# A macaron block in one kernel: row transfers placed one iteration ahead and behind the scale, group products in three rounded parts

## What is computed

```python
x = x + 0.5 * ffn(layernorm(x), gate_w, gate_b, w1, w2)
x = x + attn(layernorm(x), Wq, bq, Wk, bk, Wv, bv, Wo, bo)
x = x + 0.5 * ffn(layernorm(x), gate_w, gate_b, w1, w2)

# ffn: 32 experts, each picks 8 tokens of every batch
probs = softmax(x @ gate_w.T + gate_b, over the tokens)
vals, idx = top_k(probs, 8)                  # per batch and expert
merged = sum over the 8 picks of vals * x[idx]
o = gelu([merged, 1] @ w1) ; o = [o, 1] @ w2 # one vector per batch and expert
out[idx] += o * vals                         # back to the picked tokens

# attn: 16 heads of 32, linear and causal
q, k = exp(x @ Wq.T + bq), exp(x @ Wk.T + bk) ; v = x @ Wv.T + bv
out = (q . cumsum(k v)) / (q . cumsum(k)) ; out = out @ Wo.T + bo
```

## Time and profile before

| what | value |
|---|---|
| median of 3 runs | 2286.3 (2284.62 to 2287.34) |
| the profiled execution | 2283.05, of which its span is 2281.3 |
| gate | 0 to about 145 |
| first expert pass | about 145 to 912 |
| attention | about 912 to 1641 |
| second expert pass and the end | about 1641 to 2281 |
| TensorE busy in the span | 1962.4 (86%) |
| granted TensorE clock, mean | 0.93 |
| DMA rate where its share is full | 427 to 429 GB/s |

### The profile page before, as it was taken

How to read it: one execution, slowest core, us unless ns; L and a number is a source line. 1 busy time by engine, 2 the same in 40 slices (tenths; PEclk the granted TensorE clock), 3 DMA queues, 4 the chain that set the end, 5 groups by cost and what they waited for, 6 DMA issues and landing times.

```text
span 2281.3 us, 43539 instructions
## 1 busy us (share of the span) xinstructions
PE 1962.4 (86%) x18440; PEld 1161.6 (51%) x18440; DVE 728.5 (32%) x1235; ACT 779.3 (34%) x1413; POOL 622.9 (27%) x756
## 2 busy tenths in 40 slices
PE   5789999999999999889999999999776566656667
PEld 4546666666666666666777776777521111111111
DVE  6731111111111111367777677677410000000011
ACT  6831111121111111357777777677510000000000
POOL 7610000000000000267777777777412000000002
PEclk9999999999999999999999999999897867787777
DMA  9999999999999999776776676676499999999997
GB/s 366 357 398 404 418 401 428 430 426 422 427 418 429 418 423 415 219 261 212 250 262 224 229 249 214 198 258 209 184 406 425 427 399 428 428 428 428 428 427 332
DMA packets 133202, 804.49 MB, mean 353 GB/s; under 512 B 31240, under 2 KB 31368, under 8 KB 91792
## 3 DMA queue, kind: packets, MB, share of 16 engines
q1 hardware_dynamic: 116880, 713.29, 79.0%
q10 hardware_dynamic: 9216, 50.34, 5.3%
q0 software_dynamic: 6912, 38.07, 4.3%
HBM read 678.24 MB, written 136.95 MB: 357 GB/s over the span
## 4 chain that ended last, share of the span: by engine, by line
PE 59%; DMA 24%; ACT 5%; POOL 5%; issue 4%; SPq 1%; DVE 1%; POOLq 0%; DVEq 0%; ACTq 0%
PE ps L349 54%; DMA big<-in_L_ffn_w 22%; PE ps L353 3%; SPq L18 1%; DMA last_scratch<-idx 1%; ACT big L635 1%; POOL big L1599 1%; POOL s L1602 1%; ACT big L620 1%; PE ps L824 1%; POOL big L1572 1%; ACT big L625 1%; DMA row_scratch<-idx 1%; PE ps L512 0%; ACT big L1391 0%
## 5 line engine op out<-in xcount | busy, mean ns | idle before, releaser
L349 PE MATMUL ps<-big 128*32 128x512 f32 (+5 forms) x13568 | 946.7, 412 | 229.9 <-DMA big<-in_L_ffn_w 179.9
L349 PEld LDWEIGHTS ps<-big 128*32 128x32 f32 (+2 forms) x13568 | 374.1, 126 | 727.4 <-issue 383.6
L357 DVE TENSOR_TENSOR big<-ps,big 128x128 f32<-128x128 f32 (+4 forms) x277 | 266.7, 966 | 697.9 <-PE ps L824 511.6
L349 PE MATMUL ps<-wth,xth 128*128 128x512 f32 x768 | 311.8, 406 | 1.5 <-DVE xtl L357 1.5
L349 PE MATMUL ps<-wtl,xth 128*128 128x512 f32 x768 | 299.6, 390 | 0.0
L349 PE MATMUL ps<-wth,xtl 128*128 128x512 f32 x768 | 299.3, 390 | 0.0
L872 ACT COPY big<-ps 128x512 f32<-128x512 f32 x64 | 37.5, 586 | 644.1 <-PE ps L349 623.3
L1544 POOL TENSOR_SCALAR big<-big 128x1 f32<-128x1 f32 x8 | 1.5, 188 | 827.6 <-ACT ps L1351 827.2
L1024 DVE TENSOR_SCALAR big<-ps,big 128x512 f32<-128x512 f32 x64 | 48.1, 751 | 533.7 <-PE ps L349 533.7
L1015 ACT ACTIVATE big<-ps,big 128x512 f32<-128x512 f32 x128 | 88.2, 689 | 371.8 <-PE ps L349 356.1
L349 PE MATMUL ps<-wo,s 128*128 128x512 f32 x768 | 210.0, 408 | 3.0 <-ACT s L1436 1.4
(11 more groups left out here) (140 smaller groups left out, 1761.8 us busy)
## 6 DMA issues: line engine op xcount, KB each, us to landing
big<-in_L_ffn_w SPq DMA_DIRECT2D x254, 2048.0 KB, 35.9
p_weight_x_scratch<-big ACTq DMA_DIRECT2D x64, 768.0 KB, 11.2
big<-p_weight_x_scratch SPq DMA_DIRECT2D x64, 768.0 KB, 5.7
xt_scratch<-big SPq DMA_DIRECT2D x16, 1024.0 KB, 8.6
big<-xt_scratch SPq DMA_DIRECT2D x16, 1024.0 KB, 16.2
x_weight_scratch<-big SPq DMA_DIRECT2D x64, 256.0 KB, 3.2
out_x<-big SPq DMA_DIRECT2D x64, 256.0 KB, 4.0
big<-in_L_attn_x SPq DMA_DIRECT2D x15, 1024.0 KB, 11.3
```

The costliest lines, as they stand in the source:

```text
L349: return nc.tensor.matmul(o, l, r, start=start, stop=stop, skip_group_check=True)
L357: return nc.vector.tensor_tensor(o, p, q, op)
```

## The change

Five things are edited. First, the gathers and scatters stand behind `scale_pool` at the end of GpSimd's iteration, instead of ahead of L1599. Second, their iterations are one earlier for the first gather and for the scatters: `turn` gives 8b - 13, 8b - 12 for the gathers, 8b - 10 for the weights, 8b - 9 and 8b - 8 for the products, and 8b - 8 and 8b - 7 for the scatters; the waits of the gathers on earlier scatters follow. For batch 1 the whole chain is one or two iterations earlier: gathers at -2, weights at -1, products at 0 and 1, scatters at 0 and 1. Third, from batch 2 on the products take rounded operands: ScalarE rounds OS to OSH and VectorE forms the rest OSL (`rows_outer_act`, `rows_outer_dve`, both in iteration 8b - 11, c = 5), VectorE writes the weights rounded and their rest (GWP), and TensorE adds three products, high by high, high by low and low by high, where it had one. Fourth, TensorE's wait for ScalarE's squares stands only before the products. Fifth, the part of `rows_sp` that waits for the written row numbers and reads them back is a function of its own, `rows_read_sp`, called at expert 8.

```diff
--- before.py
+++ after.py
@@ -145,7 +145,10 @@
         assert s.at == 4 * SLOT
         TILED = 1
         G = [at(w_at + 2 * SLOT - 64 + XP * i, XP) for i in range(2)]
-        GWT = [[at(p + 128 * i, 128) for i in range(2)] for p in (m_at + 2048, os_at)]
+        GWT = [at(m_at + 2048 + 128 * i, 128) for i in range(2)]
+        OSL = [halves(f"osl{b}", os_at + 512 * b, 512) for b in range(8)]
+        OSH = [None, None] + [halves(f"osh{b}", os_at + 512 * (b - 1), 512) for b in range(2, 8)]
+        GWP = [halves(f"gwp{i}", os_at + 256 * i, 256) for i in range(2)]
         MTK = [at(m_at + 2048 + 256 * b, 256).rearrange("p (c e) -> p c e", c=8) for b in range(8)]
         RANK1, POS = at(b_at - 1024, 1024), at(os_at, 1024)
         n3 = Area(hid_at)
@@ -265,6 +268,8 @@
         s_pos, PO0 = s_ve4, NG
         s_gwT, GT0 = s_tp4, 4 * NG
         s_gwt, GW0 = s_nm4, NG
+        s_osh, OH0 = s_nma, NG + NG // 2
+        s_osl, OL0 = s_ocl, 2
         s_gc, GC0 = s_lg4, NG
         s_ga, GA0 = s_nmd, NG
         s_xst, XS0 = s_bst4, 4 * NG
@@ -277,9 +282,9 @@
         d_g, d_s = d_pick[0], d_fs
 
         def turn(n, after):
-            if n == (-1, -1, 0, 1, 2, 2, 3)[after]:
+            if n == (-2, -2, -1, 0, 1, 0, 1)[after]:
                 return 1
-            b, k = divmod(n + 12 - after, 8)
+            b, k = divmod(n + 12 - (-1, 0, 2, 3, 4, 4, 5)[after], 8)
             return b if k == 0 and 2 <= b < B else None
 
         def slot_of(g):
@@ -788,6 +793,8 @@
                         load_chunk(sp, g + ahead)
                 if p == 0 and e == 6:
                     rows_sp(sp)
+                if p == 0 and e == 8:
+                    rows_read_sp(sp)
                 if p == 1 and e == 8:
                     last_rows_sp(sp)
                 if p == 0 and e % 2 == 0 and 2 <= e // 2 + 1 < NT // 4:
@@ -1204,7 +1211,8 @@
                 pe.wait_ge(s_st, n + 1)
                 for s_ in (s_tk, s_tqv):
                     pe.wait_ge(s_, min(n + 3, 8 * TILED))
-                pe.wait_ge(s_x1sq, min(n + 3, 8 * TILED))
+                if turn(n, 3) or turn(n, 4):
+                    pe.wait_ge(s_x1sq, min(n + 3, 8 * TILED))
                 if turn(n, 2):
                     rows_weights_pe(pe, turn(n, 2))
                 for i in range(2):
@@ -1231,7 +1239,7 @@
                     for s_ in (s_tk, s_tqv):
                         pe.wait_ge(s_, min(n + 2, 8 * TILED))
                     if turn(n - 1, 2):
-                        pe.wait_ge(s_gwt, GW0 + turn(n - 1, 2) - TILED + 1)
+                        pe.wait_ge(s_gwt, gwts(turn(n - 1, 2)))
                     for k in range(2):
                         if turn(n - 1, 3 + k):
                             pe.wait_ge(s_ga, GA0 + 2 * (turn(n - 1, 3 + k) - TILED) + k + 1)
@@ -1334,7 +1342,7 @@
                     pe.wait_ge(s_xt3, n - 1)
                     bank1(n)
                     transpose4(1, PB[m % 4][:, 0, :]).then_inc(s_qtT, 1)
-                if 0 <= n < 8 * TILED - 2:
+                if -1 <= n < 8 * TILED - 2:
                     rows_turn_pe(n)
                 if live:
                     pe.wait_ge(s_kt, min(n + 2, NT))
@@ -1416,6 +1424,8 @@
                     act.wait_ge(s_x2ve, t - 1)
                     nc.scalar.activation(ps[:, 0, :], X2, ACT.Square, bias=SX2[t % 2], scale=-float(D),
                                          accum_out=SQ2[t % 2]).then_inc(s_x2sq, 1)
+                if n >= 0 and turn(n - 1, 1):
+                    rows_outer_act(act, turn(n - 1, 1))
                 if n >= 14 and c == 6:
                     merge_tokens_act(act, 8 + (n - 14) // 8, 1)
                 if n >= 5 and n % 4 == 1 and n - 2 < NT:
@@ -1511,6 +1521,8 @@
                     dve.wait_ge(d_pb[m % 4], 16 * (m // 4 + 1))
                     tt(PB[m % 4][:, 0::2, :], ps[:, 4:7:2, :], PB[m % 4][:, 0::2, :], ALU.add).then_inc(s_tqv, 1)
                     tt(PB[m % 4][:, 1, :], ps[:, 5, :], PB[m % 4][:, 1, :], ALU.add).then_inc(s_tk, 1)
+                if n >= 0 and turn(n - 1, 1):
+                    rows_outer_dve(dve, turn(n - 1, 1))
                 if turn(n, 2):
                     rows_weights_dve(dve, turn(n, 2))
                 for i in range(2):
@@ -1581,12 +1593,6 @@
                     pool.wait_ge(s_nm, n)
                     pool.wait_ge(s_qn, min(n + 2, NT))
                     nc.gpsimd.tensor_tensor(ATL, AT, ATH.bitcast(F), ALU.subtract).then_inc(s_atl, 1)
-                for i in range(2):
-                    if turn(n, i):
-                        rows_gather_pool(pool, turn(n, i), i)
-                for i in range(2):
-                    if turn(n, 5 + i):
-                        rows_scatter_pool(pool, turn(n, 5 + i), i)
                 m = n + 2
                 if m < NT:
                     j = m % 4
@@ -1606,6 +1612,12 @@
                 if 8 * TILED <= n + 3 < NT:
                     pool.wait_ge(s_kl, n + 3)
                     scale_pool(n + 3)
+                for i in range(2):
+                    if turn(n, i):
+                        rows_gather_pool(pool, turn(n, i), i)
+                for i in range(2):
+                    if turn(n, 5 + i):
+                        rows_scatter_pool(pool, turn(n, 5 + i), i)
 
 
         def rank_pool(pool):
@@ -1626,6 +1638,19 @@
                     pool.wait_ge(s_rank, 6 + 4 * h + q)
                     nc.gpsimd.memset(ROW0[h][32 * q:32 * q + 32, :], float(S * (4 * h + q) - 1)).then_inc(s_rank, 1)
 
+        def gwts(b):
+            return GW0 + 2 * b - 1
+
+        def rows_outer_act(act, b):
+            act.wait_ge(d_os[b // 4], 16 * 16)
+            act.wait_ge(s_gc, GC0 + 2 * (b - TILED))
+            act.wait_ge(s_c, 8)
+            nc.scalar.copy(OSH[b], OS[b]).then_inc(s_osh, 1)
+
+        def rows_outer_dve(dve, b):
+            dve.wait_ge(s_osh, OH0 + b - 1)
+            tt(OSL[b], OS[b], OSH[b].bitcast(F), ALU.subtract).then_inc(s_osl, 1)
+
         def rows_pool(pool):
             nc.gpsimd.iota(RANK1, [[1, S]], base=1, channel_multiplier=0,
                            allow_small_or_imprecise_dtypes=True).then_inc(s_rank1, 1)
@@ -1650,6 +1675,8 @@
             sp.wait_ge(s_pos, PO0 + 8)
             for h in range(2):
                 sp.dma_start(idxd[h], IDX1[:, 8 * h:8 * h + 8]).then_inc(d_row, 16)
+
+        def rows_read_sp(sp):
             sp.wait_ge(d_row, RW0 + 32)
             sp.dma_start(IDXG.rearrange("r (b i) -> r b i", i=2),
                          idxd.rearrange("h p j -> (h p j)").rearrange("(b r i) -> r b i", r=128, i=2)).then_inc(d_idx, 16)
@@ -1662,7 +1689,7 @@
                 pool.wait_ge(d_pst[k], 16 * (4 * b + 4))
             pool.wait_ge(s_ow, 6)
             pool.wait_ge(s_pu, 3 * NT)
-            pool.wait_ge(d_s, 32 * (b - TILED))
+            pool.wait_ge(d_s, 32 * (b - TILED) - 16 + 16 * i)
             nc.gpsimd.indirect_dma_start(
                 out=G[i], out_offset=None, in_=rowd[b],
                 in_offset=bass.IndirectOffsetOnAxis(ap=IDXG[:, 2 * b + i:2 * b + i + 1], axis=0),
@@ -1687,17 +1714,28 @@
         def rows_weights_dve(dve, b):
             dve.wait_ge(s_gwT, GT0 + b - TILED + 1)
             dve.wait_ge(s_gc, GC0 + 2 * (b - TILED))
-            if b > 1:
+            if b == 1:
+                nc.vector.tensor_copy(at(m_at + 2048, 256), ps[:, 4, 0:256]).then_inc(s_gwt, 1)
+            else:
                 dve.wait_ge(s_c, 8)
-            nc.vector.tensor_copy(at(os_at if b > 1 else m_at + 2048, 256), ps[:, 4, 0:256]).then_inc(s_gwt, 1)
+                nc.vector.tensor_copy(GWP[0], ps[:, 4, 0:256]).then_inc(s_gwt, 1)
+                dve.wait_ge(s_gwt, gwts(b) - 1)
+                tt(GWP[1], ps[:, 4, 0:256], GWP[0].bitcast(F), ALU.subtract).then_inc(s_gwt, 1)
 
         def rows_pe(pe, b, i):
-            pe.wait_ge(s_gwt, GW0 + b - TILED + 1)
+            pe.wait_ge(s_gwt, gwts(b))
             pe.wait_ge(d_os[b // 4], 16 * 16)
             pe.wait_ge(s_ga, GA0 + 2 * (b - TILED) + i)
-            for u in range(4):
-                R_ = slice(32 * u, 32 * u + 32)
-                t = mm(ps[:, 4 + u, :], GWT[b > 1][i][R_, :], OS[b][R_, :], True, True)
+            if b == 1:
+                for u in range(4):
+                    R_ = slice(32 * u, 32 * u + 32)
+                    t = mm(ps[:, 4 + u, :], GWT[i][R_, :], OS[b][R_, :], True, True)
+            else:
+                pe.wait_ge(s_osl, OL0 + b - 1)
+                for v, (w, o) in enumerate(((0, OSH[b]), (0, OSL[b]), (1, OSH[b]))):
+                    for u in range(4):
+                        R_ = slice(32 * u, 32 * u + 32)
+                        t = mm(ps[:, 4 + u, :], GWP[w][R_, 128 * i:128 * i + 128], o[R_, :], v == 0, v == 2)
             t.then_inc(s_gc, 1)
 
         def rows_add_dve(dve, b, i):
```

## The result

The changed kernel took 2292.49 us (median of 10 runs, 2290.25 to 2295.01) beside 2286.22 for the kernel before (10 runs on the same chip). The ratio is 1.0031, 95% interval 1.0023 to 1.0039: slower by about 7 us. The forecast was 4.5 us faster, with 2290 as the upper end of the range. The profiled execution took 2295.01 with a span of 2292.7. It is the longest of its ten, as the profiled one of the kernel before (2283.05) is the shortest of its ten, so that the two profiles lie 12.0 apart and the medians 6.3: the profiles say where time went, the medians how much.

What follows compares the result with a forecast made beforehand. TensorE was taken to bound the attention and DMA the second expert pass. The terms -1.0 - 5.9 - 2.0 + 2.7 + 1.7 = -4.5 us took the 2286.3 median to 2281.8, range 2275 to 2290.

Steps and rivals of the forecast that it cites:

- A: Expert 6: reading row numbers at expert 8 removes SP's wait and TensorE's 0.95 us weight wait; -1.0 us, bounds -1.0 and 0.
- B: Attention, batches 2 to 7: scatters behind the scale no longer delay the keys; 6 x 0.99 = -5.9 us, otherwise -3.
- The step that failed: GpSimd in the attention: scatters and gathers fit the 1.44 us gap after the scale; gathers were counted as costing nothing.
- C: Attention's products: three rounded sets save about 0.17 us in each of 12 groups; -2.0 us, bounds -4.6 and -0.
- that rival: Rounded products on 32 rows run one after the other, 2.76 us a group; +20.3 us, time 2304, chance 0.07.
- By that rule: Rival for the rounded products: every set shows its weight load, saving 0.8 us; time 2283, chance 0.15.
- D: ScalarE, c = 5: rounding OS costs TensorE 0.53 us in five batches; +2.7 us, bounds 0 and +3.2.
- the second step that failed: Iteration 5, batch 2: GpSimd is late and TensorE waits for it anyway, so the cast was counted as nothing.
- E: Start of the attention: moving batch 1 earlier makes TensorE wait for its gathers; +1.7 us net, bounds -1 and +6.
- the third step: Start of the attention: tile 0's scores come 7.4 us late, but most is won back, leaving +1.7.
- E +5, B -4: Rival: waits at the attention's start and GpSimd's gaps are worse than thought; time 2287.0, chance 0.15.

Runs made afterwards that it cites:

- i1: The changed kernel without ScalarE's wait for the eighth product before the cast of the outer rows; 2288.2 us, 1.0008 of the kernel before.
- f2: The changed kernel with gathers at their old place and iterations, batch 1 wholly at old iterations, the cast at 8b-14 (batch 2: 6); 2281.1 us.
- e2: The changed kernel with batch 2's rounding on ScalarE and remainder on VectorE one iteration later (6, not 5); 2288.8 us.
- f4: f2, but with batch 1 as in the changed kernel, early and behind the scale; 2284.8 us, 0.9998 of the kernel before.
- e1: The changed kernel with batch 1 at its old iterations, still behind the scale; 2295.6 us, 1.0043 of the kernel before.
- e3: The changed kernel with the edits of both e1 and e2; 2294.4 us, 1.0036 of the kernel before.
- g1: f2 with the scatters also in front of the multiplication that spreads the key scale, at their new iterations; 2276.1 us, 0.9965 of the kernel before.
- e4: The changed kernel with exact products for all batches, no cast and no remainder; 2287.4 us, 1.0006 of the kernel before.
- g2: f4 with only batch 1's gathers early, its weights, products and scatters back at old iterations; 2278.2 us, 0.9975 of the kernel before.
- g3: f2 with batch 1's weights, products and scatters one iteration later; 2287.0 us, 1.0008 of the kernel before.
- h1: f2 with VectorE's addition to the residual rows ahead of the replacement of the largest logits; 2280.3 us, 0.9973 of the kernel before.

## Why the prediction was wrong

**A, row numbers: as forecast, though not clear of the noise.** -1.0 was forecast, the wait of the earlier trace rows is gone, -1.3 between the medians was measured by itself, with an interval that takes in none.

**B, the scatters: half of it in this execution, and a loss beside it that I set to nothing.** The wait of TensorE on the keys in iteration 19 did go (the earlier trace rows had 1.16). But 6 x 0.99 took the two iterations without a scatter as the ones to be reached. By iteration pairs the gain is 0.88, 0.13, 0.15, 0.76, 0.91 and 0.14, together 3.0 for 5.9, since in three of six the addition on VectorE fell behind GpSimd's subtraction. That is a size, and not a fixed one: i1, with the scatters in the same place, has 0.73, 0.96, 0.98, 0.76, 0.68 and 0.97, together 5.1. The step that failed is the sentence that the gathers "move into the like gaps of c = 3 and c = 4, and where they stood they held up nobody". The second half was right (f2 has 10.04 in iteration 20). The first was not. The gap of the earlier trace rows was read in another iteration; in iteration 20 of the changed kernel GpSimd is 0.5 later behind the mask before the gap begins (L1608 starts 0.65 behind it, L1602 before 0.13), because the iteration ahead is now the short one, and a gather of 0.32 + 1.14 doesn't fit into what is left of 1.44. So the scale starts 0.61 later. What TensorE loses by the gather in this place takes one of two forms: in the changed kernel the row of 96 small products beside it is 0.34 longer, and the iteration 0.33; in i1 the row is as before, but TensorE waits 0.62 for the scale, and the iteration is 0.52 longer. The five iterations of this kind (12, 20, 28, 36, 44) lost 2.0 together, and 3.0 in i1. In f2, with the gathers in front, they lost at most 0.1 together.

**C, three rounded products: right.** On TensorE in iteration 23 the three sets start 0.34 and 0.23 apart:

```profile
1230.20 0.51 PE L354 MATMUL ps<-osh,gwp 32*128 32x512 f32 x4
1230.54 0.40 PE L354 MATMUL ps<-osl,gwp 32*128 32x512 f32 x4
1230.77 0.41 PE L354 MATMUL ps<-osh,gwp 32*128 32x512 f32 x4
1231.10 0.50 PE L354 MATMUL ps<-s,tri 128*128 128x512 f32 x1
```

0.90 for a group, as forecast, and -0.17 in each of twelve iterations. The sets run side by side, so that rival is out. The forecast took 0.90 between two bounds, 0.69 and 1.0, without a row for a point between them; that it was met to the hundredth is luck. The Trainium skill ("TensorE: Matmul & The Clock Gate", Part 3) says that a load overlaps with running products only in other row groups. By that rule the prediction had 0.8 in place of 2.0, with the sets 0.33 apart; they start 0.30 apart on the mean, and the kernel goes by the 2.0, so the trace bears the rule out at most in part.

**D, the cast: right for five batches, wrong for the sixth, and that is one of the two large misses.** +0.4 to +0.5 in iterations 13, 21, 37 and 45 (29 is the long one, 10.94 in e2), with L1450 as the releaser, as written; and by f2 even this was a matter of the place. The two subtractions on VectorE showed no cost. "For batch 2 it falls into n = 5, where GpSimd runs late anyway and TensorE waits for it next; I count nothing there" named the cost of the cast, 0.5, and overlooked its wait; this is the second step that failed. The wait is in the diff, for the eighth product, and the kernel's order puts that product in iteration 5 itself. Four activations and three copies stand behind it, and behind those TensorE and GpSimd: +3.7 by e2 and +4.3 by i1 between the medians, 3.2 by the profiles of both.

**E, batch 1: the mechanism was right, the net was not.** This is the third step, and the other large miss. The gather started within 0.02 of the forecast and landed 1.8 later (7.13 of wait, and 2.60 for the query's scale before it, for "about 5"); the scores came 10.0 late for 7.4. The sum then counted on 5.7 of the loss coming back. By f4 against f2, 3.7 stay by the medians (3.5 in the start, 4.6 by the ratios), for +1.7. The granted clock goes with it: 0.91 over the start in place of 0.97, and 0.94 in f4 in place of 0.98 in f2. How much of the loss it makes was not measured. The case stood among the rivals ("E +5, B -4") with 0.15.

Terms as measured: A -1.3, B -3.0, gathers +2.0, C -2.0, D +2.5 and +3.7, E +3.7: +5.6, where 5.3 to 8.9 was measured. The profile has 1.4 more in two places: iteration 58, where VectorE waits 1.37 for a load (10.51; again about 10.5 in e1, e3 and g1, and 9.65 to 9.67 in the kernel before and the nine others that left VectorE's order as it was), and 29 with the one after it (0.6 net). The terms come from different kernels, so this is as far as I divide it.

Open: why the row of 96 small products ahead of VectorE's addition is longer in some kernels. In iterations 18, 26 and 50, where a scatter is issued beside it, it takes 2.73 to 2.78 us in the changed kernel, e1 to e4 and f2 to f4, and 2.42 to 2.48 in g2, g3, h1 and i1; the addition comes about 0.3 later behind the longer one. Beside the gather of iteration 20 it takes 2.72 in the changed kernel and 2.38 in i1. The edits don't explain it: i1 differs from the changed kernel by one wait in iteration 5, and all kernels of e and f that have a transfer there are on one side, all of g, h and i that have one on the other. These ran on different chips, but no kernel was profiled on two of them, so whether it is the chip or something else that changed between them is not shown. It limits what comparisons between letters can say to about 2 us in the middle.

## What to carry to other kernels

For every wait that a change adds, look up in which iteration it is met for the first batch and not only for the later ones, and write down what is queued behind it; here one needless wait cost 3.2 us in the profile, and all the casts together 2.5. A gap on an engine is wide enough for an iteration only by that iteration's own rows: of two moves that seemed alike, one gained and one lost. When an earlier use depends on a transfer, move the transfer by as much as its user, or leave both (a transfer 2 us earlier doesn't carry a use 10 us earlier). And undo a change part by part even when its sum is a loss: g1 keeps the read, the earlier scatters and the three products, drops the gathers' move and the early batch 1, and is 8 us (5 to 11) under the kernel before. Before a small difference between two kernels is laid to an edit, look whether their iterations also differ where nothing was edited.
